# GpSimd's product of a unit's states, ordered behind the forming of the following unit's inputs

## What is computed

```python
w = jnp.exp(-jnp.exp(time_decay + jnp.tanh(xw @ td_w1) @ td_w2))   # per row and feature
r, k, v, g = ...                                                   # projections of mixed rows
def step(s, rkvw):                    # over the 128 rows of a sequence, s: 32 heads x 16 x 16
    a = k_t[..., :, None] * v_t[..., None, :]
    out = jnp.einsum('bhi,bhij->bhj', r_t, u * a + s)
    s = a + w_t[..., :, None] * s
    return (s, out)
# behind it: norm of out per head, gate g, output projection, residual, norm, feed-forward
```

## Time and profile before

| | |
|---|---|
| device time, median of 3 runs | 3896.32 us (3890.04 to 3903.24) |
| the profiled execution | 3902.75 us, span 3901.0 us |
| busy in the span: PE, DVE, ACT, POOL | 3334.0, 2001.2, 1115.5, 917.5 us |
| L1699, state products, 128 of 128x1024 | 316.2 us, mean 2471 ns |
| L1970, scans, 128 of 128x1024 | 314.3 us, mean 2456 ns |
| L1962, input products, 128 of 128x1016 | 223.4 us, mean 1745 ns |
| L1694, add_rows, 80 of 128x512 | 137.4 us, mean 1717 ns |

### The profile page before, as it was taken

How to read it: one execution, slowest core, us unless ns; L and a number is a source line. 1 busy time by engine, 2 the same in 40 slices (tenths; PEclk the granted TensorE clock), 3 DMA queues, 4 the chain that set the end, 5 groups by cost and what they waited for, 6 DMA issues and landing times. The chain is left out here.

```text
span 3901.0 us, 52045 instructions
## 1 busy us (share of the span) xinstructions
PE 3334.0 (85%) x19088; PEld 2190.8 (56%) x19088; DVE 2001.2 (51%) x2582; ACT 1115.5 (29%) x4004; POOL 917.5 (24%) x542
## 2 busy tenths in 40 slices
PE   7998799889999777766787778787769999989999
PEld 5655556556665554445565555555445555556665
DVE  4554455410000666755898989999925454610000
ACT  2343234311111454432222222222113333411111
POOL 2332223200000000004555545555400000000000
PEclk9999899989999788887888989988879999999999
DMA  4110321010001301101110111110013010010000
GB/s 149 41 35 26 116 79 47 32 52 14 19 22 35 138 23 46 40 17 53 30 37 30 33 33 33 33 33 31 25 54 121 28 41 26 26 36 27 30 32 11
DMA packets 103586, 168.85 MB, mean 43 GB/s; under 512 B 16432, under 2 KB 53936, under 8 KB 100016
## 3 DMA queue, kind: packets, MB, share of 16 engines
q1 hardware_dynamic: 98576, 123.27, 9.9%
q10 hardware_dynamic: 4896, 44.04, 2.8%
HBM read 133.72 MB, written 33.55 MB: 43 GB/s over the span
## 5 line engine op out<-in xcount | busy, mean ns | idle before, releaser
L1699 POOL TENSOR_TENSOR rec_S<-rec_S,rec_r_t 128x1024 f32<-128x1024 f32 x128 | 316.2, 2471 | 440.5 <-DVE rec_S L1970 440.5
L1970 DVE TENSOR_TENSOR_SCAN rec_S<-rec_decay,rec_S 128x1024 f32<-128x1024 f32 x128 | 314.3, 2456 | 6.6
L2131 PE MATMUL rec_p<-rec_xm,region_a 128*128 128x128 f32 x2048 | 279.2, 296 | 16.9 <-POOL rec_xm L1694 16.9
L2131 PEld LDWEIGHTS rec_p<-rec_xm,region_a 128*128 128x128 f32 x2048 | 261.1, 208 | 46.5 <-issue 35.9
L1390 PE MATMUL pmlp_bank<-pmlp_src_t,region_a 128*128 128x256 f32 x1024 | 224.9, 382 | 1.3 <-ACT pmlp_src_t L1315 1.3
L1390 PE MATMUL mlp_bank<-mlp_src_t,region_a 128*128 128x256 f32 x1024 | 224.2, 381 | 1.7 <-ACT mlp_src_t L1315 1.7
L1962 DVE TENSOR_TENSOR rec_S<-rec_vb,rec_k_t 128x1016 f32<-128x1016 f32 x128 | 223.4, 1745 | 0.0
L1402 PE MATMUL mlp_bank<-region_a,mlp_h_t 128*128 128x512 f32 x512 | 221.1, 592 | 0.0
L1402 PE MATMUL pmlp_bank<-region_a,pmlp_h_t 128*128 128x512 f32 x512 | 221.1, 592 | 0.0
L547 ACT ACTIVATE group_scores<-group_scores,group_negmax 128x128 f32<-128x128 f32 x512 | 197.4, 391 | 79.8 <-DVE group_negmax L737 79.6
L1390 PEld LDWEIGHTS pmlp_bank<-pmlp_src_t,region_a 128*128 128x128 f32 x1024 | 196.2, 192 | 31.8 <-issue 5.0
(11 more groups left out here) (310 smaller groups left out, 6421.9 us busy)
## 6 DMA issues: line engine op xcount, KB each, us to landing
rec_vb<-v_by_head SPq DMA_DIRECT2D x32, 512.0 KB, 4.1
region_a<-in_C_w ACTq DMA_DIRECT2D x2, 4096.0 KB, 18.0
region_a<-in_G_w ACTq DMA_DIRECT2D x2, 4096.0 KB, 19.3
self_x<-in_x SPq DMA_DIRECT2D x16, 256.0 KB, 3.2
self_xres<-in_x SPq DMA_DIRECT2D x16, 256.0 KB, 2.6
rows_A<-self_xres SPq DMA_DIRECT2D x16, 256.0 KB, 2.0
cross_x<-rows_A SPq DMA_DIRECT2D x16, 256.0 KB, 3.3
cross_ctx_t<-in_ctx_t SPq DMA_DIRECT2D x16, 256.0 KB, 3.3
```

What stands on the lines that cost most here:

```text
L1699: nc.gpsimd.tensor_tensor(S[u % 4][:, :, :], S[u % 4][:, :, :], bcast(r_t[:, s.k, UNITS[u][0], :], [128, JH, T], 1), ALU.mult)\
L1970: nc.vector.tensor_tensor_scan(St[:, :, :].rearrange(flat), decay[m][:, :, :].rearrange(flat), St[:, :, :].rearrange(flat), 0.0, ALU.mult, ...
L2131: last = nc.tensor.matmul(banks.bank(item)[:, f * T:(f + 1) * T], Wm[:, c, f * 128:f * 128 + 128], src[:, c, :], start=c == 0, stop=c == C ...
```

## The change

`multiply_states` gets a second wait. For unit u of sequence n it waits, beside the scan of its own unit, for `a_done` to reach the count of the unit that follows: the next unit of the sequence, or unit 0 of the next sequence behind unit 7. The last unit of the last sequence has no such wait. Nothing else is changed.

```diff
             def multiply_states(s, u):
                 pool.wait_ge(scan_done, s.n * NU + u + 1)
+                if u + 1 < NU or not (isinstance(s.n, int) and s.n == B - 1):
+
+                    pool.wait_ge(a_done, s.n * NU + u + 2)
                 nc.gpsimd.tensor_tensor(S[u % 4][:, :, :], S[u % 4][:, :, :],
                                         bcast(r_t[:, s.k, UNITS[u][0], :], [128, JH, T], 1), ALU.mult)\
                     .then_inc(prod_done, 1)
```

## The result

The changed kernel takes 4042.26 us (4 runs, 4040.03 to 4047.43) against 3895.07 for the kernel before: a ratio of 1.0378, 95% interval 1.0356 to 1.0399, slower by 147 us. Its profiled execution has a span of 4045.6 us, 144.6 more than before. Its lines are three further down from the change on: L1702 is the state product, L1965 the input product, L1973 the scan, L1952 the mix, L1916 the four multiplications.

A forecast was written before the change was run, and what follows sets the result against it. The recurrence was taken to run at the pace of VectorE's (DVE's) queue. Thirteen full steps at +9.5 us (124), +9 for the first two and +2 for the run-out gave +135, hence 4031 us, range 3990 to 4085.

The forecast's parts named there:

- The twelve lines: One pipelined step of the recurrence, cut at DVE's rows: 66.29 us before, 75.8 after, +9.5 a step.
- inputs end: The moment the next unit's inputs are formed, at the end of its input product; the delayed state product starts then.
- The chain of scan, product, addition and mix: After inputs end, scan and product exclude each other, then addition, then mix: 5.6 us; before, mostly just the scan.
- lines 3, 5 and 7: From inputs end to mixes 2, 0 and 3: 3.20, 2.33 and 2.24 us each become 5.6.
- Line 4: Mix 2 to inputs end of unit 3: 6.73 us becomes 5.5 (bounds 4.2 and 6.7); bonus values cost about 1.3.
- Line 9: Inputs end of unit 5 to mix 4: 2.24 us becomes 5.6, the mix waiting for GpSimd's addition.
- Line 1: First scan to mix 1: 14.92 us becomes 16.1, +1.2; product +2.2, bonus product +1.0, four multiplications give 2.0 back.
- rival B: Longer waits open PE gaps, bringing bursts at 1.2 GHz: one more a step +35, 4066 us, two 4101; 17%.
- Lines 10 to 12: Mix 4 through back norm and inputs end of unit 7 to next first scan: 7.48, 3.29, 10.40 become 11.2, 2.2, 9.9.
- Outside the full steps: First two steps +9 us for both (bounds 0 and 25); run-out, without mixes, +2.
- Rival A: Scan and state product run side by side: -4.2 us a step, 15 steps -63, 3833 us; 6%.

The follow-up runs named there:

- the two kernels with the wait at some units: Changed kernel with the added wait only at units 1 to 4: 4003.23 us; only at units 0, 5, 6 and 7: 3944.22 us.
- the short products: State product cut to 128 of 1024 elements per partition: in the changed kernel 3854.60 us, in the kernel before 3757.13 us.
- the kernel with sums later: Changed kernel with sums 3 to 6 one place later in PE's queue: 4024.12 us.
- the kernel with additions first: Changed kernel with GpSimd's additions and power operations queued ahead of the waiting product: 3978.90 us; same order without the added wait: 3977.63 us.
- filler matmuls: Changed kernel with extra matmuls on PE, results overwritten, in its waits for GpSimd: 4057.06 us with 25 of them, 4078.45 us with about twice as many.

## Why the prediction was right

The forecast was 4031 us in a range of 3990 to 4085, by +9.5 us for a full step; measured are 4042 and, from rows 1 and the step of the same place after, +11.2 for the one step shown, +9.9 for the mean of the 13 full ones (66.60 to 76.50). The twelve lines, as forecast, as the timeline of DVE after has them (2237.11 to 2314.64), and in the mean of the 13 full steps after:

| line | before | forecast | after | mean after |
|---|---|---|---|---|
| 1 scan 0 to mix 1 | 14.92 | 16.1 | 17.76 | 17.04 |
| 2 to inputs end 2 | 3.10 | 2.4 | 2.41 | 2.41 |
| 3 to mix 2 | 3.20 | 5.6 | 5.62 | 5.62 |
| 4 to inputs end 3 | 6.73 | 5.5 | 4.49 | 4.47 |
| 5 to mix 0 | 2.33 | 5.6 | 5.62 | 5.62 |
| 6 to inputs end 4 | 5.19 | 3.7 | 3.74 | 3.73 |
| 7 to mix 3 | 2.24 | 5.6 | 5.63 | 5.65 |
| 8 to inputs end 5 | 5.17 | 2.4 | 2.42 | 2.42 |
| 9 to mix 4 | 2.24 | 5.6 | 6.69 | 6.52 |
| 10 to the end of the back norm | 7.48 | 11.2 | 11.24 | 11.21 |
| 11 to inputs end 7 | 3.29 | 2.2 | 2.22 | 2.13 |
| 12 to the next scan 0 | 10.40 | 9.9 | 9.69 | 9.68 |

**The chain of scan, product, addition and mix** was right to 0.03 us in lines 3, 5 and 7, and shown as the cause by the two kernels with the wait at some units and by the short products. It could be sized because rows 3 held the same chain once by chance. That the total is so near is in part luck: in the mean step lines 1 and 9 are 0.9 us each above the forecast, line 4 is 1.0 below it.

**Line 4** gave back more, 2.2 us instead of 1.2. I had the bonus values fall on the small operations behind mix 2 for 2.2 us. But of the 2.24 us they took before, one was their own wait for L1962; bare they take 1.26, and end before L1998 is reached. It is the same mistake that rows 2 warn of: a recorded duration holds the stall. The 3.20 of line 3 before came from these same bonus values, not from the bonus product as the prediction has it, and by its own lines 7.8 us are given back and 17.3 lost, not 7.9 and 17.4; neither changes its sum.

**Line 9** lost 1.1 more. Mix 4 waits not for the addition but for PE, which the prediction had named as a sign of being wrong: the first half of k behind the late addition ran 3.06 us instead of 2.05, and the output rows and mix 4 stand behind it. The reason is the clock. In another step the same half took 2.05, behind an idle time of 0.96 us instead of 2.28, and there line 9 took 5.65, as forecast. This half of k in both steps, and the granted clock during each:

```profile
2282.40 3.06 PE L2134 MATMUL rec_p<-rec_xm,region_a 128*128 128x128 f32 x16 [2.28 <-POOL rec_xm L1694]
...
2511.73 2.05 PE L2134 MATMUL rec_p<-rec_xm,region_a 128*128 128x128 f32 x16 [0.96 <-POOL rec_xm L1694]
```

```profile
2282.40:2285.39 2.99, 2.99 (x16) 2.77 (x17) 2.96 (x4) 0.00 (x0) 0.51 (x1) 0.64 0.20 44
2511.72:2513.77 2.05, 2.04 (x20) 1.93 (x24) 2.05 (x3) 0.00 (x0) 0.00 (x0) 1.00 0.27 67
```

Of the 13 full steps, 11 have this half at 2.5 to 3.7 us, a clock of 0.54 to 0.78 during it, and a line 9 of 6.5 to 6.8; the other two have it at 2.05 and 2.02, a clock of 1.00, and a line 9 of 5.65 and 5.72.

**Line 1 and rival B.** Of the 13 full steps, five take 16.13 to 16.15 us from scan 0 to mix 1, the forecast's 16.1; the other eight take 17.0 to 18.2. The timeline of PE has the same operation behind the same wait in the step shown and in the next one, which is one of the five:

```profile
2244.51 2.90 PE L2157 MATMUL rec_f<-rec_base,region_a 128*128 128x128 f32 x16 [2.40 <-DVE rec_base L1916]
...
2322.03 2.12 PE L2157 MATMUL rec_f<-rec_base,region_a 128*128 128x128 f32 x16 [2.41 <-DVE rec_base L1916]
```

and the granted clock around them:

```profile
2244.51:2249.10 4.59, 4.59 (x24) 3.90 (x25) 3.87 (x3) 1.34 (x5) 2.93 (x1) 0.63 0.00 0
2318.00:2326.50 8.50, 6.09 (x43) 4.89 (x42) 8.34 (x9) 2.80 (x9) 4.50 (x2) 1.00 0.00 0
```

PE had idled 2.4 us ahead of both, but in one the clock was for a good part at the lower level, 1.2 GHz, and in the other at 2.4 GHz throughout. In all eight slower steps some of PE's work ahead of mix 1 ran at the lower level. So rival B is real: the eight steps are 11.7 us above 16.14 each in sum, and line 9 is about as much above its 5.65, together some 23 us of the 147 and of the 35 that B had for one burst a step. The stage's mean clock fell from 0.87 to 0.83, which the prediction had named as a sign for B. It came on top of the forecast instead of taking its place, and the 13 us that line 4 gave back beyond the forecast hid about half of it.

**Lines 10 to 12** held within 0.2 us in sum, with the power operation waited for 2.6 us a step and the scan of unit 7 waiting 1.7 us a step for its first column. In the kernel with sums later that wait is gone and the time 18 us lower, as it should be if sum 5 held the scan up; three other sums moved too.

**Outside the full steps** the first two lost 10.8 us (forecast 9) and the run-out behind the last sequence's first scan 7.4 (forecast 2): there each of its seven further scans and products still stands in the other's way, 45.1 us between first and last scan before, 51.6 after. Together 128.8 + 10.8 + 7.4 = 147 us, against 124 + 9 + 2 forecast.

**Rival A** is out by the short products: 97.5 us of difference where it had at most 20. What the Trainium skill's SBUF — State Buffer, section "SBUF: two separate sides", says of the two engines' shared ports fits this, the 2.50 us of the short product too. Its clause that the first to start holds them fits the changed kernel's trace: in each of the 127 pairs of a state product and the next scan, the one recorded first keeps its bare duration, whether it leads by 0.04 us or by more.

**What I had not seen** is how much of a late product can reach DVE through PE's queue. The forecast has it in lines 10 and 12. In the kernel with additions first, 54 of its 78 us go when the sums move, so most of them seem to have come by that road; the wait is not what it takes, since the same order costs 77 us without it. Against the changed kernel, opening only one road gave back 69 us (additions) or 18 (sums), both together 117. That is more than the sum of the two, which fits two roads of which each still holds DVE up when the other is open.

## What to carry to other kernels

A float32 scan with both inputs in SBUF on VectorE keeps GpSimd's product off just as a tensor_tensor does, and the recorded duration of either holds the other's run; compare the least with the median duration of a shape before believing that two operations overlap. When an instruction is made to wait, list what stands behind it in its own queue and in the queue of whoever uses its result: here a wait of one unit cost 147 us through four additions and a few sums, and moving work to where the other engine idles gave 38. GpSimd's idle time says nothing of what its work costs; here seven eighths of its products cost the kernel 142 us before the change.

## What the hardware showed unexpectedly

- Who goes first is decided by hundredths of a microsecond. In the changed kernel ten of the scans of unit 0, and five each of units 1, 2 and 3, start 0.04 to 0.05 us behind the product and stand still for 2.2 us; the other scans of units 0 to 6 start 0.04 to 0.11 us ahead and keep their 2.29. Line 3 is 5.57 us in the first case and 5.62 to 5.69 in the second, so the order hardly matters for the sum.
- The granted clock of PE didn't follow its busy time. PE was busy 926 us of a stage of 1280, then 1023 of 1291 and 1139 of 1322 with filler matmuls; the granted clock of these profiled executions was 0.83, 0.84 and 0.84. Two other executions of the last kernel had 0.929 over the whole program where this one had 0.915. Why, no run here shows.
